# Where the second attention's weights are loaded and split into half-precision parts

## The chip, the cores and the metric

The kernel runs on one core of one Trainium2 chip. The metric is the device time of one execution in microseconds (us); for the kernel before, the median of three runs is given.

## What is computed

Two transformer layers in float32 on an input of 2 x 1024 tokens with 256 features. Each layer adds to x an attention on the layer-normed x, then a feed-forward part on the layer-normed x.

- Layer 0: rotary causal attention with 16 heads of 16; a feed-forward matmul with the signs of its weights.
- Layer 1: causal attention with 16 heads of 128 (`q`, `k`, `v` each with weights and bias per head; scores divided by sqrt(128); output weights `W_O`), and a mixture of 64 experts with a shared expert.

```
q = einsum('bpd,hde->bphe', x, W_Q) + b_Q      # k and v in the same way
scores = einsum('bqhe,bkhe->bhqk', q, k) / sqrt(128)
z = einsum('bkhe,bhqk->bqhe', v, softmax(causal(scores)))
out = einsum('bqhe,hed->bqd', z, W_O) + b_O
```

The change concerns `W_Q`, `W_K`, `W_V` (per head 256 x 384 numbers together, 384 KB) and `W_O` (256 KB for two heads).

## The kernel before, in words

The program is a chain of blocks, built by `build` (L82): load, norm, projections of layer 0 (`l0_qkv`), first attention (`l0_attention`, L477), its output projection, norm, feed-forward, norm, then per batch the second attention (`l1_attention`, L865) and its output projection, then norm, router and experts. In a block each engine has its own list of instructions; engines meet by semaphores. The next block begins when all engines are through with the one before.

**Parts.** The second attention's matmuls are exact to nearly float32 by splitting each operand into two float16 parts: `hi` is the operand rounded to float16, `lo` is the operand minus `hi`. A product takes three matmuls (hi hi, hi lo, lo hi). The query columns of the weights are first multiplied by 1/sqrt(128).

**First attention.** 32 heads (2 batches x 16), taken in pairs. POOL copies a head's query and key parts together (`fetch`, L553) and its values (`fetch_values`, L570). SP turns them by transposing DMAs (`turn`, L595; the maxima's turn at L618). TensorE makes scores twice, once with queries on partitions for VectorE's maxima (L642, L755), once turned (L700) for ScalarE's exponentials (L743). Beside this stand 24 weight jobs of `l1_weights` (L797): 16 for the heads' `W_Q W_K W_V` and 8 for pairs of heads of `W_O`. Head m of the attention carries job m - 4: SP loads the float32 weights (`load`, L834, L840), POOL multiplies the query columns (L823), casts all columns (L829) and subtracts (L831), and SP stores both parts in HBM (`store`, L842, L845). POOL's list in such a head is fetch, values, the job's split, and a store of zeros for a later stage (L589). SP's list is the maxima's turn, the turns for the head after next, the job's store, the load of the next but one job.

**Norm before the second attention** (`norm`, L168, with `l1_buffers`, L1344). SP loads the parts of heads 0 and 1 (L861), the biases and both parts of `W_O` (L1367). POOL sets constants (L1372 to L1374) and scales the biases of two heads (L1379). VectorE normalizes, TensorE turns (L306), ScalarE and VectorE write the two parts of x (L291, L274).

**Second attention, one batch.** 16 heads of 8 steps each, the steps being the 8 blocks of 128 queries in the order 7, 0, 6, 1, 5, 2, 4, 3, with 1 to 8 blocks of keys. A head's steps on the engines:
- TensorE: the scores of the next step (L1052), a sixth of the next head's projections in six of the steps (`prep_pe`, L918: L924, L933), and the products with the values of five steps ago (L1073). The projections read `g.wsplit[par]`, two buffers taken in turn.
- VectorE: the reciprocal of the row sums (L1157), the next maxima (L1144), the `lo` part of a projection (L959, L962), the `lo` part of the probabilities of two steps ago (L1178).
- ScalarE: the `hi` part of a projection (L949, L952), the exponentials (L1125), the `hi` part of the last step's probabilities (L1136).
- POOL: multiplies each step's reciprocals by a constant (L1015); ScalarE's L1136 and VectorE's L1178 read the product `a_rinv`. In the second step it scales the bias of the head after next (L1006) and issues the load of that head's parts (`l1_fetch`, L857, L861).
- SP: turns the probabilities' parts by transposing DMAs (L995).

The buffers' order is that of the lists: POOL starts a step's work only when it is through with the work ahead of it in its list, and ScalarE waits at L1136 for POOL's semaphore `r_ready`. TensorE waits for weights at the first sixth of a head (`w_in`, L1093).

Of the kernel before, what the change touches and what calls it, by code (L numbers as in the profile page):

```python
# [32 lines left out]
ds = bass.ds  # L33
# [48 lines left out]
def build(nc, t_in, out):  # L82
    g = Prog()
    with ExitStack() as ctx:
# [392 lines left out]
def l0_attention(nc, g, w_begin, w_split, w_load, w_store):  # L477
# [32 lines left out]
    with ExitStack() as c:  # L510
# [29 lines left out]
        with nc.Block() as block:  # L540
            @block.gpsimd
            def _(pool):
# [39 lines left out]
                w_begin(pool)  # L582
# [11 lines left out]
            def _(sp):  # L594
# [16 lines left out]
                w_load(sp, 0)  # L611
                w_load(sp, 1)
                for m in range(NH):
# [12 lines left out]
                for i in range(2):  # L626
                    sp.wait_ge(g.s_parts[i], 16 * (WJOBS // 2))

# [165 lines left out]
WJOBS = H + H // 2  # L794


def l1_weights(g, c):  # L797

    g.w1h = g.dram("w1_parts", (H, P, 2, DC * 3 * P), F16)
    g.wo1h = g.dram("wo1_parts", (2, P, H * D), F16)  # L800
    w = [g.sb(f"pw_in{i}", [P, DC * 3 * P], F32, c) for i in range(2)]
    parts = [g.sb(f"pw_part{i}", [P, 2, DC * 3 * P], F16, c) for i in range(2)]
    scale = g.sb("pw_scale", [P, 1], F32, c)
    s_in, s_split, s_set = [g.sem(f"pw_in{i}") for i in range(2)], g.sem("pw_split"), g.sem("pw_set")
    g.s_parts = [g.sem(f"pw_out{i}") for i in range(2)]

    def width(q):
        return DC * 3 * P if q < H else 2 * D

    def done(q):  # L810

        return 3 * min(q, H) + 2 * max(q - H, 0)

    def begin(pool):
        pool.memset(scale[:, :], float(DH1) ** -0.5).then_inc(s_set, 1)
        pool.wait_ge(s_set, 1)

    def split(pool, q):
        n, at = width(q), done(q)
        pool.wait_ge(s_in[q % 2], 16 * (q // 2 + 1))  # L820
        if q < H:
            wq = w[q % 2].rearrange("p (c n) -> p c n", c=DC)[:, :, 0:P]
            pool.tensor_tensor(wq, wq, scale[:, :].unsqueeze(2).to_broadcast([P, DC, P]), ALU.mult).then_inc(s_split, 1)  # L823
            pool.wait_ge(s_split, at + 1)
            at += 1
        if q >= 2:

            pool.wait_ge(g.s_parts[q % 2], 16 * (q // 2))
        pool.tensor_copy(parts[q % 2][:, 0, 0:n], w[q % 2][:, 0:n]).then_inc(s_split, 1)  # L829
        pool.wait_ge(s_split, at + 1)  # L830
        pool.tensor_tensor(parts[q % 2][:, 1, 0:n], w[q % 2][:, 0:n], parts[q % 2][:, 0, 0:n],  # L831
                           ALU.subtract).then_inc(s_split, 1)

    def load(sp, q):  # L834
        if q >= 2:

            sp.wait_ge(s_split, done(q - 1))
        src = g.t["wqkv1"][q].rearrange("p c n -> p (c n)") if q < H else \
            g.t["wo1"][:, 2 * (q - H):2 * (q - H) + 2, :].rearrange("p h n -> p (h n)")
        sp.dma_start(w[q % 2][:, 0:width(q)], src).then_inc(s_in[q % 2], 16)  # L840

    def store(sp, q):  # L842
        sp.wait_ge(s_split, done(q + 1))
        out = g.w1h[q] if q < H else g.wo1h[:, :, (q - H) * 2 * D:(q - H + 1) * 2 * D].rearrange("a p n -> p a n")
        sp.dma_start(out, parts[q % 2][:, :, 0:width(q)]).then_inc(g.s_parts[q % 2], 16)  # L845

    return begin, split, load, store


# [7 lines left out]
def l1_fetch(g, eng, n, par, first):  # L857

    sem = g.sem("a1_w_first") if first else g.sem(f"a1_w{par}")
    head = n % H if isinstance(n, int) else n  # L860
    eng.dma_start(g.wsplit[par].rearrange("p a c n -> p (a c n)"),  # L861
                  g.w1h[ds(head, 1)].rearrange("o p a n -> (o p) (a n)")).then_inc(sem, 16)


def l1_attention(nc, g, b):  # L865
# [16 lines left out]
    w_first, w_in = g.sem("a1_w_first"), [g.sem(f"a1_w{i}") for i in range(2)]  # L882
# [19 lines left out]
    with ExitStack() as c:  # L902
# [81 lines left out]
        with nc.Block() as block:  # L984
# [14 lines left out]
            def _(pool):  # L999
                def next_weights(n, par):  # L1000

                    pool.wait_ge(g_ready, n * NCH + NCH)
                    ahead = n - (N0 - 2) if isinstance(n, int) else n + (2 - N0)
                    hb = ahead % H if isinstance(n, int) else ahead
                    pool.wait_ge(g_lo, n * NCH + NCH)
                    pool.tensor_tensor(g.bias[par][:, :], g.bqk[:, ds(hb, 1), :].rearrange("p o q -> p (o q)"),  # L1006
# [337 lines left out]
def l1_buffers(nc, g, c2):  # L1344
# [15 lines left out]
    def loads(sp):  # L1360
        for n in range(2):
            l1_fetch(g, sp, n, n, True)
# [689 lines left out]
```

## Time and profile before

| what | us |
|---|---|
| median of 3 runs | 1561.48 |
| runs | 1561.48, 1565.09, 1559.58 |
| span of the profiled execution (first to last instruction) | 1556.1 |
| TensorE busy (PE) | 1394.1, 90% of the span |
| VectorE busy (DVE) | 1047.9, 67% |
| ScalarE busy (ACT) | 814.5, 52% |
| GpSimd busy (POOL) | 374.1, 24% |

The profile gives one execution; its own device time is not listed apart from the span, which leaves out what lies before the first and after the last instruction. PE is TensorE's matmuls, PEld its weight loads, SP the queue that issues most DMAs. Lines such as L831 are those of the kernel before. "idle before" is the time an engine stood still ahead of an instruction, with what ended that wait. The granted clock (PEclk) is 1.00 at 2.4 GHz and 0.50 at 1.2 GHz.

### The profile page before, as it was taken

The numbers are of one execution on the slowest core, as the hardware profiler recorded it, in microseconds if no ns is written. First come the engines' busy times: TensorE is split into PE (matmuls) and PEld (weight loads), VectorE is DVE, ScalarE is ACT, GpSimd is POOL, SyncE is SP. The second block draws the span as 40 slices with busy tenths as digits, with TensorE's granted clock in tenths as the row PEclk, the third lists the DMA queues.
The fourth block names the chain that finished last, engine by engine and source line by source line (L and its number), as shares of the span: only waits on it lengthen the run. The fifth ranks groups of instructions, "written<-read, shape, count | busy, mean of one in ns | idle before, by whom it ended". The sixth has DMA issues, their size and how long they took to land. (4 is left out here: it accounts for less than half of the span.)

```text
span 1556.1 us, 36410 instructions
## 1 busy us (share of the span) xinstructions
PE 1394.1 (90%) x12869; PEld 982.9 (63%) x12869; DVE 1047.9 (67%) x2191; ACT 814.5 (52%) x1682; POOL 374.1 (24%) x796
## 2 busy tenths in 40 slices
PE   3848999999679999999989999999998798799977
PEld 2414555554556777777777677777767745599963
DVE  4856777764778888888822888888882378422228
ACT  1316665655327877777711877787770116222330
POOL 0434665530021111111110101111101000577730
PEclk9969999999889999999999999999999799799985
DMA  3038999872025655565620665566651430599948
GB/s 101 1 68 170 248 246 248 214 160 52 1 79 113 143 138 138 133 142 133 138 59 1 129 141 134 135 142 138 138 128 31 133 95 1 162 290 288 289 135 295
DMA packets 463401, 215.08 MB, mean 138 GB/s; under 512 B 412082, under 2 KB 434448, under 8 KB 463072
## 3 DMA queue, kind: packets, MB, share of 16 engines
q1 hardware_dynamic: 448992, 175.09, 47.0%
q0 software_dynamic: 12000, 36.90, 8.0%
q10 hardware_dynamic: 2336, 2.16, 0.4%
q8 instruction: 39, 0.64, 0.2%
q14 instruction: 34, 0.28, 0.1%
HBM read 81.97 MB, written 31.52 MB: 73 GB/s over the span
## 5 line engine op out<-in xcount | busy, mean ns | idle before, releaser
L1073 PE MATMUL bank<-a_pt,v_part 128*128 128x128 f16 x3456 | 235.3, 220 | 13.9 <-DMA a_pt<-a_ph 8.9
L1136 ACT ACTIVATE a_ph<-a_p,a_rinv 128x1024 f16<-128x1024 f32 (+7 forms) x256 | 198.7, 777 | 79.3 <-POOL a_rinv L1015 75.7
L755 DVE TENSOR_REDUCE a_qh<-bank 128x1 f16<-128x1024 f32 (+7 forms) x256 | 182.3, 755 | 85.0 <-PE bank L645 83.3
L1073 PEld LDWEIGHTS bank<-a_pt,v_part 128*128 128x128 f16 x3456 | 208.9, 98 | 47.2 <-DVE z_part L1163 7.5
L1144 DVE TENSOR_REDUCE a_negm<-bank 128x1 f32<-128x1024 f32 (+7 forms) x256 | 191.7, 749 | 55.9 <-PE bank L1057 55.7
L1052 PE MATMUL bank<-a_k,a_q 128*128 128x512 f16 (+3 forms) x1152 | 228.7, 326 | 0.2
L743 ACT ACTIVATE a_p<-bank 128x1024 f32<-128x1024 f32 (+7 forms) x256 | 157.8, 649 | 128.7 <-PE bank L700 113.3
L1178 DVE SCALAR_TENSOR_TENSOR a_ph<-a_p,a_rinv,a_ph 128x1024 f16<-128x1024 f32 (+7 forms) x256 | 206.8, 808 | 1.7 <-ACT a_ph L1136 1.7
L1125 ACT ACTIVATE a_p<-bank,a_negm 128x1024 f32<-128x1024 f32 (+7 forms) x256 | 189.3, 739 | 21.6 <-DVE a_negm L1144 21.6
L1015 POOL TENSOR_TENSOR a_rinv<-a_rinv,p_scale 128x1 f32<-128x1 f32 x256 | 48.8, 191 | 610.6 <-DVE a_rinv L1157 610.4
L924 PE MATMUL bank<-x_part,wsplit 128*128 128x512 f16 x768 | 186.0, 379 | 4.1 <-PEq L199 1.8
L642 PE MATMUL bank<-a_k,a_q 128*128 128x512 f16 (+3 forms) x384 | 108.6, 340 | 33.8 <-DMA a_k<-a_kh 18.9
L1052 PEld LDWEIGHTS bank<-a_k,a_q 128*128 128x128 f16 x1152 | 99.3, 98 | 60.7 <-ACT a_p L1125 1.2
L700 PE MATMUL bank<-a_qm,a_k 128*128 128x512 f16 (+3 forms) x384 | 112.3, 331 | 6.9 <-ACT a_p L743 5.2
L924 PEld LDWEIGHTS bank<-x_part,wsplit 128*128 128x128 f16 x768 | 69.7, 98 | 71.4 <-issue 4.0
L1760 POOL DMA_INDIRECT x_rows<-token_rows,src x64 | 62.3, 973 | 170.0 <-issue 167.9
L1811 PE MATMUL bank<-x_T,wgu 128*88 128x96 f32 x1024 | 96.1, 247 | 0.7 <-issue 0.7
L933 PE MATMUL bank<-wsplit,x_part 128*128 128x128 f16 x1536 | 95.9, 219 | 0.8 <-DVE a_k L959 0.5
L1811 PEld LDWEIGHTS bank<-x_T,wgu 128*88 128x88 f32 x1024 | 92.6, 158 | 4.4 <-issue 0.9
L933 PEld LDWEIGHTS bank<-wsplit,x_part 128*128 128x128 f16 x1536 | 88.2, 98 | 5.7 <-DVE a_k L959 2.1
L1929 DVE TENSOR_TENSOR x_h<-bank,x_sg 88x192 f32<-88x192 f32 x64 | 22.7, 354 | 94.4 <-ACT x_sg L1888 94.4
L1206 PE MATMUL bank<-wo_part,z_part 128*128 128x256 f16 x768 | 84.2, 273 | 1.7 <-PEq L984 1.7
(206 smaller groups left out, 2230.9 us busy)
## 6 DMA issues: line engine op xcount, KB each, us to landing
wgu<-in_wgu SPq DMA_DIRECT2D x64, 352.0 KB
choice_rows<-zero POOLq DMA_DIRECT2D x24, 512.0 KB, 4.9
c_rows<-choice_rows SPq DMA_DIRECT2D x16, 768.0 KB, 11.2
wsplit<-w_parts POOLq DMA_DIRECT2D x30, 384.0 KB, 3.8
wd<-in_wd SPq DMA_DIRECT2D x64, 176.0 KB
pw_in<-in_wqkv SPq DMA_DIRECT2D x16, 384.0 KB, 4.9
w_parts<-pw_part SPq DMA_DIRECT2D x16, 384.0 KB, 2.9
a_pt<-a_ph SPq DMA_TRANSPOSE x256, 3.0
```

What stands on the lines that cost most here:

```text
L700: ins = pe.matmul(ST[k % 2][:, c4 * 512:c4 * 512 + w_], kT[s][:, kb, :], queries[:, kb * P + c4 * 512:kb * P + c4 * 512 + w_], start=True, ...
L743: act.activation(pT[s][:, off[kb]:off[kb + 1]], ST[k % 2][:, 0:(BT - kb) * P], ACT.Exp).then_inc(e_ready, 1)
L755: dve.tensor_reduce(qh[s][:, i, MC:MC + 1], s1_place(t), AX.X, ALU.max, negate=True).then_inc(m_ready, 1)
L924: ins = pe.matmul(G_ps[k % 2], w[:, a, c_, (k // 2) * P:(k // 2 + 1) * P], g.xs[x_][:, c_, b * S + (k % 2) * 512:b * S + (k % 2 + 1) * 512 ...
L933: ins = pe.matmul(G_ps[k % 2][:, j * P:(j + 1) * P], g.xs[x_][:, c_, t * P:(t + 1) * P], w[:, a, c_, 2 * P:3 * P], start=(c_ == 0 and (a, ...
L1052: ins = eng.matmul(ps[:, c4 * 512:c4 * 512 + w_], qT[par][a][:, i * P:(i + 1) * P], kT[par][k_][:, c4 * 512:c4 * 512 + w_], start=(a, k_) ...
L1073: ins = eng.matmul(Z_ps[:, cols], g.vs[par][v_][:, k, :], turned[slot][:, a * blocks[j] + k, :], start=(k == 0 and (v_, a) == PARTS[0]), s ...
L1125: eng.activation(probs[j % NBUF][:, 0:w_], S_ps[j % 4][:, 0:w_], ACT.Exp, bias=negm[:, par, j:j + 1], accum_out=rsum[:, par, j:j + 1]).the ...
L1136: eng.activation(parts[slot][:, 0:w_], probs[slot][:, 0:w_], ACT.Copy, scale=rinv[:, p_, jj:jj + 1]).then_inc(p_hi, 1)
L1144: eng.tensor_reduce(negm[:, par, j:j + 1], S_ps[j % 4][:, 0:blocks[j] * P], AX.X, ALU.max, negate=True).then_inc(m_ready, 1)
L1178: eng.scalar_tensor_tensor(parts[slot][:, w_:2 * w_], probs[slot][:, 0:w_], rinv[:, p_, jj:jj + 1], parts[slot][:, 0:w_], ALU.mult, ALU.su ...
L1811: ins = pe.matmul(b_[:, m * C:(m + 1) * C], g.wgu[s][:, c_, m * MH:(m + 1) * MH], xeT[(s // 2) % 2][:, s % 2, c_, :], start=(c_ == 0), sto ...
```

## The change

The 24 weight jobs leave the first attention, with the two tensors in HBM that held the parts. The second attention loads the float32 weights itself and splits them on POOL. Two raw buffers `g.wraw` (float32, 384 KB each) and one `g.woraw` (256 KB) are new.

- In the norm before the second attention POOL issues the loads of heads 0 and 1 and of the first pair of `W_O`, splits both heads, issues the loads of heads 2 and 3, and scales the biases. SP loads only the biases.
- In the second attention POOL, behind the product of step j of head n, splits slice j of head n + 2, for the first six steps. A slice is 128 of the 768 columns: a cast and a subtraction, and in slices 0 and 3 (query columns) a product first. In the first eight heads of the first batch, steps 6 and 7 split each one half of a pair of `W_O`. After the eighth step POOL scales the bias of head n + 2 and issues the load of head n + 4, and in the first heads that of the next pair of `W_O`.
- TensorE waits for the slices' semaphore `s_wready` in place of the DMA's.
- POOL's loop over pairs of heads is written out.

```diff
-                with ExitStack() as cw:
-                    l0_attention(nc, g, *l1_weights(g, cw))
+                l0_attention(nc, g)
...
                 for m in range(4, NH):
                     fetch(m)
                     fetch_values(m - 2)
-                    if m - 4 < WJOBS:
-                        w_split(pool, m - 4)
...
                     if m + 2 < NH:
                         turn(m + 2)
-                    if 0 <= m - 3 < WJOBS:
-                        w_store(sp, m - 3)
-                        if m - 1 < WJOBS:
-                            w_load(sp, m - 1)
...
+def l1_fetch(g, eng, n):
+
+    eng.dma_start(g.wraw[n % 2][:, :], g.t["wqkv1"][n % H].rearrange("p c n -> p (c n)")).then_inc(g.s_wraw[n % 2], 16)
+
+
+def l1_split(g, pool, n, k):
+
+
+    c_, part = divmod(k, 3)
+    raw = g.wraw[n % 2][:, k * P:(k + 1) * P]
+    dst = [g.wsplit[n % 2][:, a, c_, part * P:(part + 1) * P] for a in range(2)]
+    if k == 0:
+        pool.wait_ge(g.s_wraw[n % 2], 16 * (n // 2 + 1))
+    if part == 0:
+        pool.tensor_tensor(raw, raw, g.bscale[:, 0:1].to_broadcast([P, P]), ALU.mult).then_inc(g.s_wsc, 1)
+        pool.wait_ge(g.s_wsc, DC * n + c_ + 1)
+    pool.tensor_copy(dst[0], raw).then_inc(g.s_whi, 1)
+    pool.wait_ge(g.s_whi, 3 * DC * n + k + 1)
+    pool.tensor_tensor(dst[1], raw, dst[0], ALU.subtract).then_inc(g.s_wready, 1)
...
             @block.gpsimd
             def _(pool):
...
+                for n in range(N0, N0 + H):
                     for j in range(BT):
...
+                        pool.wait_ge(r_raw, n * BT + (j + 1))
+                        pool.tensor_tensor(rinv[:, n % 2, j:j + 1], rinv[:, n % 2, j:j + 1], g.pscale[:, :],
+                                           ALU.mult).then_inc(r_ready, 1)
+                        if n + 2 < B * H and j < 3 * DC:
+                            if j == 0:
+
+                                pool.wait_ge(g_ready, (n + 1) * NCH)
+                            l1_split(g, pool, n + 2, j)
+                        if b == 0 and n < OJOBS and j >= 3 * DC:
+                            l1_split_out(g, pool, n, j - 3 * DC)
+                    if n + 2 < B * H:
+
+                        pool.wait_ge(g_lo, (n + 1) * NCH)
+                        pool.tensor_tensor(g.bias[n % 2][:, :], g.bqk[:, (n + 2) % H, :], g.bscale[:, :],
+                                           ALU.mult).then_inc(b_ready, 1)
+                    if n + 4 < B * H:
+                        pool.wait_ge(g.s_wready, 3 * DC * (n + 3))
+                        l1_fetch(g, pool, n + 4)
+                    if b == 0 and n + 1 < OJOBS:
+                        pool.wait_ge(g.s_wosplit, 4 * (n + 1))
+                        l1_fetch_out(g, pool, n + 1)
...
-                            if k == 0 and which == "first" and b == 0:
-                                eng.wait_ge(w_first, 32)
-                            elif k == 0:
-
-                                eng.wait_ge(w_in[1 - par], n * 8 + (8 - 8 * (1 - par)))
+                            if k == 0:
+                                eng.wait_ge(g.s_wready, n * (3 * DC) + 2 * 3 * DC)
...
     def loads(sp):
-        for n in range(2):
-            l1_fetch(g, sp, n, n, True)
         sp.dma_start(g.bqk[:, :, :], g.t["b_QK"]).then_inc(s_in, 16)
         sp.dma_start(g.bv[:, :], g.t["b_V"]).then_inc(s_in, 16)
         sp.dma_start(g.bo[:, :], g.t["b_O"].partition_broadcast(P)).then_inc(s_in, 16)
-        for a in range(2):
-            sp.dma_start(g.wo1p[a].rearrange("p h n -> p (h n)"), g.wo1h[a]).then_inc(s_wo, 16)
-        sp.wait_ge(s_wo, 32)
+        sp.wait_ge(s_in, 48)
...
         pool.wait_ge(s_set, 3)
 
+        for n in range(2):
+            l1_fetch(g, pool, n)
+        l1_fetch_out(g, pool, 0)
+        for n in range(2):
+            for k in range(3 * DC):
+                l1_split(g, pool, n, k)
+        pool.wait_ge(g.s_wready, 2 * 3 * DC)
+        for n in range(2):
+            l1_fetch(g, pool, n + 2)
         pool.wait_ge(s_in, 48)
```

## Rows read from the trace of the kernel before

**Rows 1.** Busy time by stretch: length; PE, PEld, DVE, ACT, POOL; clock; DMA.

```profile
117.00:335.00 218.00, 203.01 (x2035) 108.62 (x2033) 155.23 (x271) 131.20 (x218) 120.47 (x243) 1.00 0.93 223
...
470.00:800.00 330.00, 320.20 (x3544) 235.50 (x3543) 270.71 (x506) 252.14 (x506) 36.30 (x160) 0.99 0.60 134
```

**Rows 2.** Waits in steady heads of the second attention, first batch, 500 to 745.

```profile
ACT a_ph L1136 <- POOL a_rinv L1015: 30.2, 24, 1.4
DVE a_negm L1144 <- PE bank L1057: 21.4, 36, 0.9
...
POOL wsplit L861 <- issue: 5.6, 12, 0.7
```

**Rows 3.** Waits in the first attention, 117 to 335, then SP's queue's own.

```profile
PE bank L700 <- DMA a_qm<-a_qh: 0.3, 1, 0.3
...
SPq L845 <- POOL pw_part L831: 2.0, 5, 0.5
```

**Rows 4.** Timeline of ScalarE: first exponential of three heads, two pairs apart.

```profile
303.25 1.02 ACT L743 ACTIVATE a_p<-bank 128x1024 f32<-128x1024 f32 x1 [0.23 <-PE bank L700]
...
337.30 1.02 ACT L743 ACTIVATE a_p<-bank 128x1024 f32<-128x1024 f32 x1 [0.23 <-PE bank L700]
...
371.23 1.02 ACT L743 ACTIVATE a_p<-bank 128x1024 f32<-128x1024 f32 x1
```

**Rows 5.** Timeline of the norm before the second attention and the first matmul behind.

```profile
443.00 0.10 POOL L1372 MEMSET bscale<- 128x1 f32 x1 [4.44 <-POOLq L1313]
...
450.86 0.58 POOL L1379 TENSOR_TENSOR bias<-bqk,bscale 128x2 f32<-128x2 f32 x2 [7.70 <-DMA bo<-in_b_O]
...
451.51 6.02 DVE L274 TENSOR_TENSOR x_part<-bank,x_part 128x256 f16<-128x256 f32 x16
...
457.85 1.46 PE L924 MATMUL bank<-x_part,wsplit 128*128 128x512 f16 x6 [1.80 <-PEq L199]
```

**Rows 6.** POOL's DMAs of line 861: issue (ns), and time to landing.

```profile
L861 POOL DMA_DIRECT2D wsplit<-w_parts x30: 563/563/585, 471.6 to 1116.6; - x30
...
DMA to landing us min/median/max: 2.9/3.8/5.4
```

**Rows 7.** POOL's groups by shape: busy us, mean ns, idle before.

```profile
L823 POOL TENSOR_TENSOR pw_in<-pw_in,pw_scale 128x256 f32<-128x256 f32 x16 | 9.7, 607 | 26.5 <-DMA pw_in<-in_wqkv 26.5
...
L831 POOL TENSOR_TENSOR pw_part<-pw_in,pw_part 128x512 f16<-128x512 f32 x8 | 9.2, 1151 | 0.7
...
L575 POOL COPY a_vh<-v 128x128 f32<-128x128 f32 x32 | 9.1, 286 | 66.7 <-PE bank L663 66.7
```

**Rows 8.** Timeline of POOL in one weight job.

```profile
205.90 0.82 POOL L829 CAST pw_part<-pw_in 128x768 f16<-128x768 f32 x1
206.81 1.64 POOL L831 TENSOR_TENSOR pw_part<-pw_in,pw_part 128x768 f16<-128x768 f32 x1
```

**Rows 9.** Busy time by stretch, as rows 1, and TensorE's timeline at 787.98.

```profile
456.30:459.70 3.40, 1.85 (x9) 0.91 (x10) 1.13 (x4) 0.73 (x3) 0.00 (x0) 1.00 0.03 7
...
787.40:790.80 3.40, 2.82 (x27) 2.85 (x28) 1.08 (x2) 0.00 (x0) 0.00 (x0) 0.50 0.92 208
...
787.98 1.33 PE L1073 MATMUL bank<-a_pt,v_part 128*128 128x128 f16 x11 [2.76 <-DMA a_pt<-a_ph]
```

**Rows 10.** Timeline of VectorE in a steady head.

```profile
575.42 0.15 DVE L1157 RECIPROCAL a_rinv<-a_rsum 128x1 f32<-128x1 f32 x1
...
576.35 0.34 DVE L1178 SCALAR_TENSOR_TENSOR a_ph<-a_p,a_rinv,a_ph 128x128 f16<-128x128 f32 x1
...
577.44 0.56 DVE L1144 TENSOR_REDUCE a_negm<-bank 128x1 f32<-128x384 f32 x1 [0.68 <-PE bank L1057]
```

**Rows 11.** Line 428 on VectorE (ns min/median/max), one instance, POOL's line 459 beside it.

```profile
L428 DVE TENSOR_TENSOR qk_parts<-rot,qk_parts x32: 411/422/1491, 42.7 to 90.1; 128x256 f16<-128x256 f32 x32
...
87.66 1.48 DVE L428 TENSOR_TENSOR qk_parts<-rot,qk_parts 128x256 f16<-128x256 f32 x1
...
87.48 1.37 POOL L459 TENSOR_TENSOR rot<-rot 128x512 f32<-128x512 f32 x1 [1.82 <-DVE rot L442]
```

More of the change, by code:

```diff
@@ L621, in _ @@
                         turn(m + 2)
-                    if 0 <= m - 3 < WJOBS:
-                        w_store(sp, m - 3)
-                        if m - 1 < WJOBS:
-                            w_load(sp, m - 1)
-                for i in range(2):
-                    sp.wait_ge(g.s_parts[i], 16 * (WJOBS // 2))
             def max_scores(pe, t, m, s):
@@ L789, in _ @@
                 z_out(NP - 1, NH - 2)
[L794 to L847, printed above, removed]
+OJOBS = H // 2
 LAG = 5
@@ L854, with l1_fetch_out, l1_split_out @@
 NCH = 6
[L857 to L862, printed above, removed]
+def l1_fetch(g, eng, n):
[12 more added lines that the diff above has]
+    pool.tensor_tensor(dst[1], raw, dst[0], ALU.subtract).then_inc(g.s_wready, 1)
+def l1_fetch_out(g, eng, q):
+    eng.dma_start(g.woraw[:, :], g.t["wo1"][:, 2 * q:2 * q + 2, :].rearrange("p h n -> p (h n)")).then_inc(g.s_wo, 16)
+def l1_split_out(g, pool, q, k):
+    raw = g.woraw[:, k * D:(k + 1) * D]
+    dst = [g.wo1p[a][:, 2 * q + k, :] for a in range(2)]
+    if k == 0:
+        pool.wait_ge(g.s_wo, 16 * (q + 1))
+    pool.tensor_copy(dst[0], raw).then_inc(g.s_wosplit, 1)
+    pool.wait_ge(g.s_wosplit, 4 * q + 2 * k + 1)
+    pool.tensor_tensor(dst[1], raw, dst[0], ALU.subtract).then_inc(g.s_wosplit, 1)
 def l1_attention(nc, g, b):
@@ L881, in l1_attention @@
     pt_in = [g.sem(f"a1_turned{i}") for i in range(NBUF)]
-    w_first, w_in = g.sem("a1_w_first"), [g.sem(f"a1_w{i}") for i in range(2)]
     N0 = b * H
@@ L999, in _ @@
             def _(pool):
[L1000 to L1006, printed above, removed]
-                                       g.bscale[:, :], ALU.mult).then_inc(b_ready, 1)
-                    l1_fetch(g, pool, hb, par, False)
@@ L1010, in head @@
-                def head(eng, n, par, which, more):
-                    for j in range(BT):
-                        if j == 1 and more:
-                            next_weights(n, par)
-                        eng.wait_ge(r_raw, n * BT + (j + 1))
-                        eng.tensor_tensor(rinv[:, par, j:j + 1], rinv[:, par, j:j + 1], g.pscale[:, :],
-                                          ALU.mult).then_inc(r_ready, 1)
-                head(pool, N0, 0, "first", True)
-                head(pool, N0 + 1, 1, "first", True)
@@ L1020, in _ @@
-                with pool.Fori(1, H // 2 - 1) as pair:
-                    for par in range(2):
-                        head(pool, pair * 2 + (N0 + par), par, "mid", True)
-                for par in range(2):
-                    head(pool, N0 + H - 2 + par, par, "last", b + 1 < B)
+                for n in range(N0, N0 + H):
+                    for j in range(BT):
+                        pool.wait_ge(r_raw, n * BT + (j + 1))
[17 more added lines that the diff above has]
+                        l1_fetch_out(g, pool, n + 1)
@@ L1357, in l1_buffers @@
     g.bvp = g.sb("bv_part", [P, 2, H], F16, c2)
-    s_in, s_set, s_wo, b_ready = g.sem("l1_in"), g.sem("l1_set"), g.sem("l1_wo"), g.sem("a1_bias")
+    g.wraw = [g.sb(f"w_raw{i}", [P, DC * 3 * P], F32, c2) for i in range(2)]
+    g.woraw = g.sb("wo_raw", [P, 2 * D], F32, c2)
+    g.s_wraw = [g.sem(f"a1_w_in{i}") for i in range(2)]
+    g.s_wsc, g.s_whi, g.s_wready = [g.sem(f"a1_w_{n}") for n in ("scaled", "hi", "ready")]
+    g.s_wo, g.s_wosplit = g.sem("l1_wo"), g.sem("l1_wo_split")
+    s_in, s_set, b_ready = g.sem("l1_in"), g.sem("l1_set"), g.sem("a1_bias")
     def loads(sp):
-        for n in range(2):
-            l1_fetch(g, sp, n, n, True)
         sp.dma_start(g.bqk[:, :, :], g.t["b_QK"]).then_inc(s_in, 16)
```

11 lines of the change are left out of this document (3 added, 8 removed).

## The prediction

> **What bounds the kernel now.** I read the stages first (busy time by stretch), then the waits inside the two attentions, then the timeline where the change sits. Times below are of the one profiled execution, span 1556.1 us; the median of the runs is 1561.48 us, 5.4 us more. That rest (launch and end) is taken as unchanged, so a difference found in the profile is added to 1561.48. A difference under 0.3% (4.7 us) cannot be told from none here: the three runs alone spread over 5.5 us.
>
> TensorE is the limit of both attentions: busy 203.0 of 218 us while the first one carries the weight jobs, and 320.2 of 330 us in the first batch of the second [rows 1]. In the second attention's steady heads the list of waits has no TensorE entry at all; what waits is ScalarE for POOL's `a_rinv` (30.2 us in 24 waits over 12 heads) and VectorE for TensorE's scores (21.4 us, 1.8 us a head) [rows 2]. Those two are slack behind a saturated TensorE. So work moved between POOL, SP and the DMA queues changes the time only if it makes TensorE wait, or stands in the short norm between the FFN and the second attention, where TensorE has little to do.
>
> **First attention: jobs removed.** Gone are 24 loads and 24 stores on SP, 16 products, 24 casts and 24 subtractions on POOL. None was in TensorE's way: it waited once, 0.3 us, for a turned maximum, and SP's queue waited for POOL's splits 2.0 us in all [rows 3]. What the jobs cost is read from the pace. Two pairs of heads with jobs start at 303.25 and end at 337.30, 34.05 us; the next two, without, run to 371.23, 33.93 us [rows 4]. That is 0.06 us a pair, over 12 pairs 0.7 us at most if all carry it. I take -0.3 us; bounds 0 and -1.1 (a few turned maxima landed late early in the stage). The zero-filling stores of POOL's queue stay; they are issued earlier, because POOL no longer waits for a job's load ahead of them.
>
> **Norm before the second attention: work added.** Before, SP fetches ready parts and POOL has three memsets and two bias products. After, POOL issues three DMAs, splits two heads (6 slices each), issues two more DMAs and makes the biases, all inside the norm's block; the next block starts when every engine is through. The prices:
> - POOL starts at 443.0 [rows 5]; three memsets and their wait, 0.2 us.
> - Landing: a POOL DMA of 384 KB takes 0.563 us to issue and 2.9 to 5.4 us, median 3.8, to land [rows 6]. First weights at 443.2 + 3.8 = 447.0. The other two land behind it, under cover of head 0's slices.
> - A slice has 128 columns. Cast: the 128x128 copy, 0.29 us. Subtraction: 1.64 us for 768 columns (206.81) and 1.15 us for 512 give 0.49 us per 256, so 0.41 us for 128. Product: 0.61 us for 256 less 0.25, 0.36 us. From a cast's end (205.90 + 0.82) to the subtraction that waits for it at 206.81 is 0.09 us [rows 7, 8].
> - A head: 6 x 0.29 + 6 x 0.41 + 2 x 0.36 = 4.92 us, six such gaps and two behind products +0.7, less about 0.4 where a subtraction's end and the next cast, which wait for nothing, overlap (estimate); so 5.2 us; two heads 10.5 us. Splits end at 457.5.
> - Two DMA issues 1.1 us, two bias products 0.6 us [rows 5]: POOL ends at 459.2.
>
> VectorE ended this norm at 457.53 and TensorE started at 457.85 [rows 5], so the change of blocks takes 0.3 us. POOL becomes last, by 1.7 us: TensorE starts at about 459.5. Bounds: landing at 446.1, no gaps and cheap slices give +0.3 us; landing at 448.6, slices a tenth dearer and 0.4 us before each of five issues (12 issues idled 5.6 us in the steady heads) give +6.2 us [rows 2, 6]. I take +1.7, since each term has a row of its own size.
>
> What this trace has of such landings was 2.9 to 5.4 us [rows 6]. The Trainium skill's page "DMA: Bandwidth & Descriptors", section on the anatomy of one SWDGE DMA, fits 2.0 us plus bytes over 436 GB/s for a DMA from GpSimd's queue. By that estimate 384 KB takes 2.9 us, the rows' lowest and not their median, and the start would be 0.9 us late instead of 1.7.
>
> **TensorE's clock after the longer pause.** Before, TensorE stops at 456.05, starts again 1.80 us later and is at 2.4 GHz from 456.3 to 459.7 [rows 5, 9]. With the start at 459.5 the pause becomes 3.5 us. After a pause of 2.76 us near the end of the first batch the clock stood at 1.2 GHz from 787.4 to 790.8 [rows 9]. I expect the same here: 3.4 us at half rate lose 1.7 us of matmul work, of which 0.3 us hides in waits for evacuation; +1.4 us. Bounds 0 (no fall) and +3.4 (two such stretches).
>
> **Second attention: slices beside the heads.** Before, a head has on POOL 8 `a_rinv` products, one bias and one DMA. After, for 30 heads six slices (0.8 us, or 1.2 with the product) come on top, one behind each of the first six `a_rinv`; in the first eight heads two half slices of the output weights (1.1 us) and a DMA. Who waits for POOL's queue is ScalarE, at the next `a_rinv`. VectorE's reciprocals come closest around the 128-column instance of line 1178: one starts at 575.42, the next follows that instance, which ends at 576.69 [rows 10]. In these 1.2 us slice 2 (0.8 us) fits. Behind the last `a_rinv` of the first eight heads half slice, bias and two issues need some 3.7 us against 2.0 us to the next reciprocal, so the next head's first `a_rinv` comes about 1.7 us late; ScalarE has 2.5 us a head of waiting for POOL to give (30.2 by 12) [rows 2]. New weights are ready a whole head (some 20 us: 330 by 16 [rows 1]) before TensorE asks, so the new wait costs nothing. In steady heads: 0 us. In the last head of the first batch TensorE does wait, for turned probabilities; slices there may delay VectorE by 0.1 to 0.4 us. I take +0.3, bounds 0 and +1.0.
>
> **Sum:** -0.3 + 1.7 + 1.4 + 0.3 = +3.1 us, 1564.6 us.
>
> **Rivals.**
> (A) The slices stall VectorE. The trace has such a stall: the subtraction of line 428, both inputs in SBUF, takes 0.41 us by itself and 1.48 us when it starts at 87.66 in the middle of POOL's 87.48 to 88.85; it ends at 89.14, 0.29 us after POOL's end [rows 11]. Line 1178, eight times a head, has two SBUF inputs as well. By my replay of one head, slice 2's subtraction (576.2 to 576.6) meets the one that starts at 576.35 and holds it by 0.1 us; the half slices of the first eight heads hold two more, 0.5 us together. VectorE's next idle gap, 0.68 us at 577.44, takes the first up [rows 10]. The point that decides is 1.8 us a head: with more stall than VectorE's idle time, scores come late. If none of it were absorbed, 30 x 0.1 + 8 x 0.5 = 7 us come on top: 1571.6. For it speaks the stall, against it the idle gap behind each collision. Chance 0.13.
> The Trainium skill's page "SBUF — State Buffer", section "Who interferes with whom", has the same stall as a rule: the read port that both engines use is locked for a whole instruction. It speaks against this change, and for cutting the work into slices.
> (B) The first attention gains more. All that could be won is TensorE's 15.0 us of idle time there [rows 1]; a third of it would be -5 us and, with a norm that costs +0.3, give 1556.8. Against it: those gaps alternate with VectorE and ScalarE, and the pairs without jobs keep the pace [rows 4]. Chance 0.07.
> (C) The norm hides POOL's work after all (early landing, no fall of the clock): -0.3 + 0.3 + 0.3 = +0.3, 1561.8. Chance 0.20.
> (D) My forecast, 1564.6: chance 0.60; its own range 1560 to 1569.
>
> **How the numbers follow.** The lows sum to -0.8 us and the highs without (A) to +10.6 us; with the scatter of a median of a few runs the range is 1559.5 to 1570. Faster by over 0.3% is (B), 0.07. Slower by over 0.3% is (A) with its 0.13 and the upper end of (D), where landing and clock both go badly, 0.13: 0.26. The rest, 0.67, is no change that can be told.
>
> **What the new profile would show.** Right: pairs in the first attention still 17 us apart; TensorE's first matmul of the second attention 1 to 3 us later after the norm's start, with POOL the last engine in the norm; 1.2 GHz granted for some 3 us at that start; heads as far apart as before with no TensorE wait; line 1178 instances 0.1 to 0.4 us longer at places. Wrong: TensorE waiting for scores' evacuation in the steady heads, heads longer by 0.1 us or more, a start more than 6 us late, or pairs below 16.8 us.

## The result and the profile after

The kernel after takes 1587.71 us (median of four runs, 1587.25 to 1588.44) against 1562.57 us of the kernel before (four runs): ratio 1.0168, 95% interval 1.0149 to 1.0186. Forecast was 1564.6, range 1559.5 to 1570. The profiled span grew from 1556.1 to 1585.8 us, by 29.7. That is 4.6 us more than the medians differ. Where a run lists both, its time is 1.6 to 1.9 us above its span, so the profiled execution of the kernel before was faster than any of its four timed runs. Differences of stages, taken from the profiles, overstate the loss by these 4.6 us. The head of the page after:

```profile
span 1585.8 us, 36456 instructions
...
PE 1404.9 (89%) x12869; PEld 984.9 (62%) x12869; DVE 1053.6 (66%) x2191; ACT 815.4 (51%) x1682; POOL 489.7 (31%) x1221
```

GpSimd carries 116 us more than before, but it is idle two thirds of the span; what the kernel lost is TensorE standing still or running slowly. Five stages, cut at the same instructions in every kernel, show where. "First attention" runs from its first GpSimd memset to the first exponential of its last head; "norm" from the norm's first VectorE instruction to TensorE's first matmul of the second attention; "start" from there to the first exponential; heads 1 and 2 of the first batch; "tail" from the first exponential of that batch's last head to the second batch's first. "Total" is the timed median, the rest are us of the profiled execution.

| kernel | total | span | first attention | norm | start | heads 1, 2 | tail |
|---|---|---|---|---|---|---|---|
| before | 1562.57 | 1556.1 | 287.4 | 14.8 | 11.6 | 20.2, 20.2 | 86.0 |
| after | 1587.71 | 1585.8 | 298.7 | 23.0 | 13.8 | 21.5, 21.4 | 90.5 |
| e1_spacers | 1574.36 | 1572.6 | 287.6 | 21.8 | 13.2 | 20.2, 21.8 | 90.8 |
| e2_zeros_early | 1578.02 | 1576.2 | 286.0 | 23.0 | 14.0 | 21.7, 21.9 | 91.3 |
| e3_fetch_later | 1580.87 | 1579.1 | 296.5 | 18.8 | 14.0 | 21.7, 21.7 | 88.8 |
| e4_tail_fetch | 1581.29 | 1579.5 | 296.0 | 22.5 | 13.7 | 21.6, 21.7 | 86.0 |
| e5_wo_moved | 1583.95 | 1582.1 | 296.3 | 22.6 | 14.0 | 20.2, 21.0 | 90.3 |
| e6_head1_later | 1576.22 | 1574.4 | 297.1 | 15.7 | 11.6 | 20.2, 21.5 | 90.8 |
| e7_all_moved | 1560.89 | 1559.8 | 285.3 | 15.7 | 13.2 | 20.8, 20.7 | 86.0 |
| e8_before_in_twos | 1568.45 | 1566.8 | 294.6 | 14.8 | 11.6 | 20.2, 20.2 | 85.9 |
| e9_even_stores | 1576.94 | 1575.2 | 286.0 | 23.1 | 14.0 | 21.6, 21.8 | 90.9 |
| e10_odd_stores | 1576.47 | 1574.7 | 286.6 | 22.9 | 13.9 | 21.6, 21.6 | 90.4 |
| e11_all_moved_2 | 1568.1 | 1565.3 | 285.8 | 15.5 | 12.9 | 20.5, 20.1 | 90.1 |
| e13_before_zeros_early | 1559.8 | 1557.0 | 285.2 | 14.4 | 12.9 | 20.2, 20.2 | 86.3 |

e7, e11 and e13 were run 12, 6 and 12 times, e1 to e6 and e8 to e10 once each, beside a kernel before of 1564.33 us (e1 to e4), 1563.21 us (e5, e6) and 1560.87 us (e8 to e10). From before to after: first attention +11.3, norm +8.2, start +2.1, heads 1 and 2 +2.5, tail +4.5, together 28.6; the other 1.1 us is for the most part the scatter of code that is the same in both (the first stages alone +1.2). Where the code of the first attention is that of after (after, e3 to e6), it took 296.0 to 298.7 us, so a difference under 3 us means little there: in the profile of after one odd head took 13.5 us where the others took 10.1 to 10.4, and 1.2 GHz stood from 155.0 to 158.4; e3 to e6 have no such head. The totals of e1, e3, e4, e5 and e6 came out 1 to 3 us below what was expected of them; in e3 to e6 the first attention alone gave 1.6 to 2.7 us against the profile of after.

Busy time by stretch in the kernel after, columns as [rows 1]: the two attentions, then the start of the second and the tail of its first batch.

```profile
118.10:346.00 227.90, 205.95 (x2024) 107.98 (x2022) 154.31 (x269) 131.19 (x216) 55.99 (x178) 0.99 0.68 143
...
492.00:822.00 330.00, 316.98 (x3496) 231.23 (x3494) 273.85 (x505) 252.58 (x506) 137.86 (x423) 0.99 0.64 140
...
472.40:482.70 10.30, 4.59 (x11) 1.61 (x12) 0.75 (x1) 0.69 (x1) 1.92 (x6) 0.50 0.23 79
813.80:820.60 6.80, 4.79 (x45) 4.19 (x41) 0.00 (x0) 0.00 (x0) 0.00 (x0) 0.50 0.71 157
```

TensorE's idle time in the first attention went from 15.0 us [rows 1] to 22 (227.90 less 205.95), although the DMA share there fell from 0.93 to 0.68. In the last two stretches the granted clock is 0.50 (1.2 GHz).

**First attention.** Waits of the kernel after, 117 to 345 (us in total, times, longest):

```profile
POOL a_qh L563 <- DMA a_k<-a_kh: 94.0, 14, 10.5
...
DVE a_qh L743 <- PE bank L633: 70.2, 89, 3.5
...
PE bank L630 <- DMA a_k<-a_kh: 9.1, 11, 2.3
```

TensorE now waits 9.1 us for turned keys, in 11 waits. The kernel before has one such wait of 1.7 us (its 117 to 335; it stands beside the turned maximum of [rows 3]):

```profile
PE bank L642 <- DMA a_k<-a_kh: 1.7, 1, 1.7
```

What changed is when the 512-KB zero stores leave GpSimd. The timeline before, then after (start, issue time):

```profile
198.78 0.59 POOL L589 DMA_DIRECT2D choice_rows<-zero  x1
...
208.39 0.59 POOL L589 DMA_DIRECT2D choice_rows<-zero  x1
...
218.10 0.59 POOL L589 DMA_DIRECT2D choice_rows<-zero  x1
```

```profile
201.23 0.53 POOL L585 DMA_DIRECT2D choice_rows<-zero  x1
...
203.39 0.53 POOL L585 DMA_DIRECT2D choice_rows<-zero  x1
...
219.20 0.53 POOL L585 DMA_DIRECT2D choice_rows<-zero  x1
```

Before, one store per head, here 9.6 and 9.7 us apart. After, two 2.2 us apart and then a pause: before an even head's values GpSimd waits for TensorE, and the odd head has nothing of that kind. The weight jobs had held the second store back. SyncE's transposes of the odd head meet both; DMA issues of the kernel after, then of e9 (half of the stores), 160 to 325, KB each and median us to landing:

```profile
choice_rows<-zero POOLq DMA_DIRECT2D x18, 512.0 KB, 5.3
a_qm<-a_qh SPq DMA_TRANSPOSE x18, 3.9
a_q<-a_qh SPq DMA_TRANSPOSE x18, 5.2
a_k<-a_kh SPq DMA_TRANSPOSE x18, 4.4
```

```profile
choice_rows<-zero POOLq DMA_DIRECT2D x10, 512.0 KB, 4.5
a_qm<-a_qh SPq DMA_TRANSPOSE x20, 3.8
a_q<-a_qh SPq DMA_TRANSPOSE x20, 4.2
a_k<-a_kh SPq DMA_TRANSPOSE x19, 3.8
```

The medians are over even and odd heads: in the kernel after an even head's query transpose lands in 3.3 us, an odd head's in 7.1, with one store (e9) in 5.0. TensorE waits for the key transpose, the last of three. From 130 to 335 us it had landed 5.8 to 6.6 us after SyncE began the first of the three in an even head, and in an odd head 9.1 to 9.4 us (once 10.9). With one store it was 7.3 to 8.5 (e9) and 7.6 to 8.9 (e10). TensorE waited for turned keys in each of the eleven odd heads of the kernel after and in none of e9 and e10. From the even head's first exponential to the odd head's it is 10.1 to 10.4 us in the kernel after (once 13.5) and 9.1 to 9.4 in the kernel before: this is the odd head's time in the expectations below.

**Norm.** GpSimd's timeline in the kernel after, then TensorE's, then the block-end instruction of GpSimd's queue (ns min/median/max, start):

```profile
455.42 0.10 POOL L1331 MEMSET p_scale<- 128x1 f32 x1
457.76 1.15 POOL L793 DMA_DIRECT2D w_raw<-in_wqkv  x2 [2.24 <-issue]
...
461.26 0.50 POOL L805 TENSOR_TENSOR w_raw<-w_raw,bscale 128x128 f32<-128x128 f32 x1 [1.71 <-DMA w_raw<-in_wqkv]
...
472.50 0.43 POOL L809 TENSOR_TENSOR wsplit<-w_raw,wsplit 128x128 f16<-128x128 f32 x1
473.23 1.12 POOL L793 DMA_DIRECT2D w_raw<-in_wqkv  x2 [0.30 <-POOL wsplit L809]
474.36 0.36 POOL L1345 TENSOR_TENSOR bias<-bqk,bscale 128x2 f32<-128x2 f32 x2
```

```profile
478.11 1.44 PE L887 MATMUL bank<-x_part,wsplit 128*128 128x512 f16 x3 [8.83 <-PEq L198]
```

```profile
L198 POOLq DRAIN  x1: 4110/4110/4110, 473.7 to 473.7; - x1
```

GpSimd stands still for 2.24 us ahead of its first DMA, splits until 472.93, and its drain lasts from 473.7 to 477.8: the second of the two fetches begun at 473.23 (its own issue at 473.81) lands 3.77 us later, at 477.58. VectorE's own part had ended at 470.76.

**Steady heads.** Waits over twelve heads, 552 to 794; they answer to [rows 2]:

```profile
ACT a_ph L1091 <- POOL a_rinv L966: 27.0, 22, 1.4
DVE a_negm L1099 <- PE bank L1015: 19.8, 30, 0.9
```

27.0 and 19.8 us, against 30.2 and 21.4. The heads stay 20.18 to 20.47 us apart. VectorE's `lo` parts of the probabilities did get longer at three of their eight widths (mean 989 ns against 874 at 640 columns, 672 against 607 at 384, 380 against 342 at 128), some 0.2 us a head, and the heads did not.

### The profile page after: what moved, and what is told of

It is laid out like the page before. It is cut to its first block and busy times, and to the rows that moved or that the text cites. A ratio compares the mean times of both kernels' runs of the same rounds, so it can differ in the third digit from the quotient of the medians.

```text
span 1585.8 us, 36456 instructions
## 1 busy us (share of the span) xinstructions
PE 1404.9 (89%) x12869; PEld 984.9 (62%) x12869; DVE 1053.6 (66%) x2191; ACT 815.4 (51%) x1682; POOL 489.7 (31%) x1221
## 5 line engine op out<-in xcount | busy, mean ns | idle before, releaser
L1031 PE MATMUL bank<-a_pt,v_part 128*128 128x128 f16 x3456 | 236.5, 220 | 18.0 <-DMA a_pt<-a_ph 10.5
L1134 DVE SCALAR_TENSOR_TENSOR a_ph<-a_p,a_rinv,a_ph 128x1024 f16<-128x1024 f32 (+7 forms) x256 | 211.1, 825 | 1.7 <-ACT a_ph L1091 1.7
L1080 ACT ACTIVATE a_p<-bank,a_negm 128x1024 f32<-128x1024 f32 (+7 forms) x256 | 189.2, 739 | 21.4 <-DVE a_negm L1099 21.4
L887 PEld LDWEIGHTS bank<-x_part,wsplit 128*128 128x128 f16 x768 | 70.3, 98 | 79.8 <-issue 13.9
L809 POOL TENSOR_TENSOR wsplit<-w_raw,wsplit 128x128 f16<-128x128 f32 x192 | 83.1, 433 | 15.4
```

Of the source, the lines that this page charges most:

```text
L887: ins = pe.matmul(G_ps[k % 2], w[:, a, c_, (k // 2) * P:(k // 2 + 1) * P], g.xs[x_][:, c_, b * S + (k % 2) * 512:b * S + (k % 2 + 1) * 512 ...
L1031: ins = eng.matmul(Z_ps[:, cols], g.vs[par][v_][:, k, :], turned[slot][:, a * blocks[j] + k, :], start=(k == 0 and (v_, a) == PARTS[0]), s ...
L1080: eng.activation(probs[j % NBUF][:, 0:w_], S_ps[j % 4][:, 0:w_], ACT.Exp, bias=negm[:, par, j:j + 1], accum_out=rsum[:, par, j:j + 1]).the ...
L1134: eng.scalar_tensor_tensor(parts[slot][:, w_:2 * w_], probs[slot][:, 0:w_], rinv[:, p_, jj:jj + 1], parts[slot][:, 0:w_], ALU.mult, ALU.su ...
```

## The experiments

All but e8 and e13 start from the kernel after. Theory Z: zero stores in pairs. Theory N: GpSimd's chain and drain in the norm. Theories W and T: raw fetches that meet the transposes of the probabilities, in heads 1 and 2 and in the tail. The expectations of e1 and e2 count the first attention up to the norm's first instruction: 351.3 us before, 362.2 after.

**e1_spacers.** GpSimd's splits (product, cast, subtraction) come back on a buffer of ones, without their loads and stores.

```
+                w_begin(pool)
                 for m in range(4, NH):
                     fetch(m)
                     fetch_values(m - 2)
+                    w_split(pool, m - 4)
                     pool.dma_start(zv[m - 4], g.zero[:, :])
```

> The kernel after, with GpSimd's 24 splits put back into the first attention on a buffer of ones, without their loads, stores and load waits (their results are used by nobody). Theory Z (the zero stores now leave GpSimd in pairs about 2.2 us apart, where the splits held them 8 to 10 us apart, and meet the transposing DMAs of the odd heads): the splits space the stores again, so the odd heads' transposes land in 3.2 to 3.6 us instead of 5 to 7, and the first attention goes from 362.2 us back to 351 to 353; total 1577 to 1579. Rival L (the splits' loads and stores, or the waits on them, kept something else in order, or the first attention is longer for a reason that has nothing to do with the stores): the first attention stays at 360 to 364 us and the total at 1585 to 1589. Rival G (GpSimd time is scarce): slower than the kernel after.

First attention 287.6 us (352.6 up to the norm), total 1574.36, 2.6 us under the expected range. Doing useless work is 13 us faster than doing none, 11 of it in this stage: what the jobs gave the kernel before was the distance between stores. Spaced stores still meet transposes, which from 175 us on take up to 5.2 us to land and not only 3.2 to 3.6, but TensorE waits for none of them there. L falls, G too.

**e2_zeros_early.** The stores go to the QKV projection.

```
                 for t in range(NT):          # l0_qkv, GpSimd
                     ...
+                    for z in range(2 * t, min(2 * t + 2, ZD)):
+                        pool.dma_start(zv[z], g.zero[:, :]).then_inc(g.s_zero, 16)
```

> The kernel after, with the 24 zero stores issued from GpSimd's loop of the first QKV projection (two per token tile) in place of the first attention. Theory Z: no store is left to meet the transposes, so the first attention goes from 362.2 us to 349 to 351.5 (a head pair of 17.85 us falls to 17.0 or less), the QKV stage grows by 0 to 2 us, total 1575 to 1578. Rival L (not the stores): the first attention stays at 360 to 364 us, total 1585 to 1589.

286.0 us (351.0 up to the norm), with the QKV stage no longer (the first attention begins at 92.89, after: 92.93). The stores, not the jobs' removal in itself, cost the 11 us.

**e3_fetch_later.**

```
-        pool.wait_ge(g.s_wready, 2 * 3 * DC)     # scales(), in the norm
-        for n in range(2):
-            l1_fetch(g, pool, n + 2)
+                if b == 0:                        # l1_attention, GpSimd, first thing
+                    pool.wait_ge(g.s_wready, 2 * 3 * DC)
+                    for n in range(2):
+                        l1_fetch(g, pool, n + 2)
```

> The kernel after, with the two fetches of heads 2 and 3 moved out of the norm's GpSimd list to the beginning of the second attention's. Theory N (the norm's end waits in GpSimd's drain for these two fetches to land, 473.7 to 477.8 us): the 1.1 us of issuing and the 3.1 us of the drain go, the stretch from the norm's first VectorE instruction to the first attention matmul falls from 23.0 to 18.5 to 20 us, total lower by 3 to 4.5 us (1583 to 1585). Rival M (the drain waits for something else, or the matmul for the biases): 23.0 us as before, total unchanged at 1587 to 1589.

Norm 18.8 us, 4.2 less: theory N, M falls. The total was 6.8 us lower; 2.2 of it is the scatter of the first attention, 1.7 the tail, whose code is the same.

**e4_tail_fetch.** Head 19's raw fetch waits for the second batch.

```
-                    if n + 4 < B * H:
+                    if n + 4 < B * H and n != H - 1:
...
+                if b == 1:
+                    pool.wait_ge(g.s_wready, 3 * DC * (H + 2))
+                    l1_fetch(g, pool, H + 3)
```

> The kernel after, with the last raw fetch of batch 0 (head 19's, issued 810.7 us, landing 5.1 us later) moved to the start of the second batch's GpSimd list. Theory T (that fetch meets the last transposes of the probabilities of batch 0): from head 15's first exponential to the second batch's first, 90.5 us falls to 86 to 87, total lower by 3.5 to 4.5 us (1583 to 1584.5). Rival U (the tail's extra time is the GpSimd slices, or the clock alone): 90 to 91 us, total unchanged. Rival V (the fetch meets the second batch's first transposes instead): 90.5 us falls, but the first heads of the second batch take 1 to 4 us more.

Tail 86.0 us, as before, and the second batch's heads unchanged: theory T. The fetch, 16.2 us into the last head, meets two transposes of the probabilities: they take 5.3 and 5.1 us to land, the same two in e4 2.7 and 3.0. The waits of TensorE's matmuls in the tail, after (806 to 828), then e4 (804 to 826):

```profile
PE bank L1031 <- DVE z_part L1118: 2.9, 2, 2.4
...
PE bank L1031 <- DMA a_pt<-a_ph: 2.8, 2, 2.0
```

```profile
PE bank L1034 <- DMA a_pt<-a_ph: 3.4, 2, 2.6
...
PE bank L1034 <- DVE z_part L1121: 0.6, 1, 0.6
```

Together 5.7 us against 4.0. The other 2.8 us of the 4.5 go with the clock: 1.2 GHz was granted for 10.2 us of the kernel after's tail (two stretches, 813.8 to 820.6 and 824.0 to 827.4, with 8.2 us of matmuls in them), for 3.4 us of e4's and of the kernel before's (3.0 and 2.8 us of matmuls). What such a fall costs was not tried apart from the waits.

**e5_wo_moved.**

```
-                    if b == 0 and n + 1 < OJOBS:      # end of head n
+                        if b == 0 and 0 < n < OJOBS and j == 2:
                             l1_fetch_out(g, pool, n)
```

> The kernel after, with the fetch of the output weights (256 KB) issued behind the third block of a head in place of directly behind the 384-KB fetch at the end of the head before. Theory W (heads 1 and 2 of the first batch take 21.4 to 21.5 us because two fetches 0.6 us apart meet the transposes of the head's first blocks): both return to 20.2 to 20.6 us, total lower by 1.5 to 2.6 us. Rival X (one fetch alone at that place is enough, or the loop's first passes are the cause): both stay above 21.2 us. Rival Y (the moved fetch meets other transposes): heads 1 and 2 fall, but heads 3 to 7 rise above 20.6 us each.

Head 2 takes 21.0 us; in every run without this edit that splits in the second attention it took 21.4 to 21.9. Head 1's 20.2 proves less, since it was also 20.2 in e1 and e6. Part of W, then: the 384-KB fetch alone keeps some of the cost. Nor does the place of the fetches alone decide it: heads 3 to 7 of the kernel after have the same two, also 2.4 and 3.0 us behind the head's first exponential, and take 20.2 to 20.5 us. What differs is how late a transpose of the probabilities lands. Head 1 (508 to 520), then head 3 (551 to 563), of the kernel after:

```profile
DMA to landing us min/median/max: 2.3/3.9/7.4
```

```profile
DMA to landing us min/median/max: 2.4/3.1/6.0
```

With 7.4 us TensorE stood still for 1.1 us; with 6.0 to 6.4 us (heads 3 to 7) it had no pause of 0.2 us. In head 1 of e1 and e6, whose fetches stand at the same place, the longest took 5.9 and 6.1 us. Why the same fetches delay the transposes of heads 1 and 2 more is open.

**e6_head1_later.**

```
-        for n in range(2):                        # scales()
-            for k in range(3 * DC):
-                l1_split(g, pool, n, k)
+        for k in range(3 * DC):
+            l1_split(g, pool, 0, k)
+                if b == 0:                        # l1_attention, GpSimd, first thing
+                    for k in range(3 * DC):
+                        l1_split(g, pool, 1, k)
+                    pool.wait_ge(g.s_wready, 2 * 3 * DC)
+                    for n in range(2):
+                        l1_fetch(g, pool, n + 2)
```

> The kernel after, with the norm's GpSimd list cut to head 0's slices: head 1's six slices and the fetches of heads 2 and 3 move to the beginning of the second attention's list. Theory N (GpSimd's chain of landing, twelve slices, two issues and a drain sets the norm's end): 5.8 us of slices and the 4 us of the fetches go from it, until VectorE's own part ends last; from the norm's first VectorE instruction to the first attention matmul 23.0 us falls to 15 to 17 us (before: 14.8), and the matmul stands at 468 to 472 in place of 478.1 with an undisturbed first attention counted as after's; total lower by 6 to 9 us. Rival M (the matmul waits for something else at the norm's end): 20 us or more. Rival P (head 1's slices now hold up the start of the attention): the norm falls, but from the matmul to the first exponential, 13.75 us, it rises by 2 us or more, or head 0 takes over 18 us.

Norm 15.7 us, start 11.6, head 0 16.6 us long (after: 17.1): theory N again, without P. GpSimd, VectorE and TensorE at the end of this norm:

```profile
467.64 0.35 POOL L1347 TENSOR_TENSOR bias<-bqk,bscale 128x2 f32<-128x2 f32 x2
```

```profile
464.54 5.83 DVE L273 TENSOR_TENSOR x_part<-bank,x_part 128x256 f16<-128x256 f32 x16
```

```profile
470.69 1.02 PE L887 MATMUL bank<-x_part,wsplit 128*128 128x512 f16 x4 [1.93 <-PEq L198]
```

GpSimd is through at 468.0 and VectorE at 470.37, as it was last in [rows 5]. The 0.9 us over the kernel before lies in VectorE's 16 normalizing instructions, here and in the kernel before (busy us, mean ns):

```profile
L265 DVE TENSOR_SCALAR n_xnb<-x,mean,rstd 128x256 f32<-128x256 f32 x16 | 6.4, 472 | 0.0
```

```profile
L266 DVE TENSOR_SCALAR n_xnb<-x,mean,rstd 128x256 f32<-128x256 f32 x16 | 5.3, 406 | 0.0
```

They take 0.40 to 0.41 us (once 0.47) until GpSimd's first split begins at 461.23, and 0.51 to 0.65 us beside the splits; GpSimd's casts take 0.37 to 0.49 us there and 0.29 later. So the slices did meet VectorE, in the norm. This is read from the timeline; no run kept the two apart.

**e7_all_moved** is e2, e4, e5 and e6 together.

> The kernel after with four edits together: zero stores in the QKV projection, head 1's slices and the fetches of heads 2 and 3 behind the norm, the output weights' fetch behind the third block of a head, the last raw fetch of batch 0 at the start of the second batch. If the four meetings and waits are all of the loss: first attention 286 us from its start to the last head's first exponential, norm as in the kernel before to within 2 us, heads 1 and 2 at 20.2 to 20.6, tail of batch 0 at 86, total 1558 to 1566 us, a ratio to the kernel before of 0.997 to 1.002. If something else remains, or the parts meet again elsewhere: 1567 us or more. If less GpSimd and DMA work in the first attention was worth something in itself: below 1558.

1560.89 us (12 runs) against 1563.21 (17 runs), ratio 0.9987, interval 0.9973 to 1.0001. Heads 1 and 2, at 20.8 and 20.7, stay above the expected range. The 25 us are gone, and what is left cannot be told from the kernel before.

**e8_before_in_twos** starts from the kernel before.

```
-                    if m - 4 < ZD:
-                        pool.dma_start(zv[m - 4], g.zero[:, :])
+                    if m - 4 < ZD and m % 2:
+                        for z in (m - 5, m - 4):
+                            pool.dma_start(zv[z], g.zero[:, :])
```

> The kernel before, untouched but for its zero stores: the store of an even head waits for the odd head's and the two leave together, behind the odd head's split. Theory Z in its burst form (two 512-KB stores at once are what slows a transposing DMA): the transposes that meet a pair land in 5 to 7 us, and the first attention grows from 287.4 us (its start to the last head's first exponential) by 3 to 11 us. Theory Z in its phase form (what counts is that a store leaves GpSimd just as SyncE begins an odd head's transposes; behind the splits it falls between two heads): unchanged to 1 us, 287 to 289 us.

294.6 us, 7.2 more, with nothing else of the change in it; one head of it took 11.9 us, with 1.2 GHz from 251.1 to 254.5. The cost is uneven: the first pairs of stores fall between transposes and cost nothing, from 240 us on they meet them (key transpose issued at 240.9: 8.7 us to landing, and TensorE waited 2.8 us for it). So both forms hold a part: it takes two stores, and they must meet the transposes.

**e9_even_stores, e10_odd_stores.** Half of the stores stay in the first attention, the other half goes to the QKV projection.

```
-                    if m - 4 < ZD:
+                    if m - 4 < ZD and m % 2 == 0:     # e10: m % 2 == 1
```

> The kernel after with half of its zero stores: the twelve of the odd heads are issued in the QKV projection, the twelve of the even heads (the first of each pair) stay. Burst form: no two stores meet, so the odd heads take 9.3 to 9.5 us and the first attention 286 to 288 us. Phase form: one store at that place still slows the odd heads to 9.7 to 10.2 us, first attention 291 to 299 us.

> The kernel after with the other half: the twelve of the even heads are issued in the QKV projection, the twelve of the odd heads (the second of each pair, some 2 us behind the first) stay. Burst form: odd heads 9.3 to 9.5 us, first attention 286 to 288 us. Phase form: 9.7 to 10.2 us, 291 to 299 us; if this run is long and that with the even stores is not, the phase is that of the second store, on top of the query and key transposes.

286.0 and 286.6 us. Each store of a pair is free by itself at the place where the two cost 0.9 us a head: burst, not phase.

**e11_all_moved_2** is e7 with both fetches of a head inside the next one.

```
+                        if n and n + 3 < B * H and j == 2:
+                            l1_fetch(g, pool, n + 3)
+                        if b == 0 and 0 < n < OJOBS and j == 4:
+                            l1_fetch_out(g, pool, n)
```

> As the run with four edits together, but both fetches of a head are issued inside the next head: the raw weights behind its third block, the output weights behind its fifth (the last raw fetch of batch 0 falls into the second batch by this). If the fetch at a head's first blocks is what is left in heads 1 and 2 (20.7 us each there): 20.2 to 20.4 us each, and the total 1 to 2 us below the 1560.9 of that run, ratio to the kernel before 0.996 to 0.999. If not: heads 1 and 2 at 20.6 or more, total as there.

Heads 1 and 2 at 20.5 and 20.1, but 1568.1 us, ratio 1.0041 (1.0025 to 1.0058): a miss. The tail is 90.1 us and the second batch's first two heads take 2.3 us more than in e7. The fetch in the first batch's last head, at 778.7, now meets that head's transposes, and the clock falls to 1.2 GHz three times between 785 and 803. A place that is free in a steady head is not free in a first or last one.

**e13_before_zeros_early** is the kernel before with e2's edit.

> The kernel before with its 24 zero stores issued in the QKV projection; the weight jobs stay. If the stores, spaced by the splits, cost the kernel before nothing: first attention 287 to 287.6 us, total unchanged, ratio 0.999 to 1.001, and what the run with four edits has over the kernel before comes from the weight jobs' removal. If they cost something there too: first attention 285 to 286.5 us, ratio 0.998 to 0.9995, and moving them is worth as much without the change.

First attention 285.2 us; 1559.8 us, ratio 0.9989 (0.9976 to 1.0003). Spaced stores may cost the kernel before some 2 us, at the edge of what can be told. With the weight jobs in place it is as fast as e2's and e7's first attention without them.

## Why the prediction was wrong

- **First attention, -0.3 us: wrong, and the largest error.** The failing step is the sentence that the zero-filling stores "stay; they are issued earlier", priced at nothing. Issued earlier meant issued in twos; measured +11.3 us in the profiles (8.6 to 9.7 in e3 to e6), and e1, e2, e8, e9 and e10 put it on the pairs. The bounds, 0 and -1.1, held no loss at all, since only removed instructions were priced and not what their waits did to the DMAs behind them. That the jobs themselves cost TensorE nothing was right: with the stores away, 285.2 us with jobs (e13) and 286.0 without (e2). Rival (B) falls with it. The reading that TensorE waited once, 0.3 us, left out the wait of 1.7 us for turned keys at 127.3, the kind that grew to 9.1.
- **Norm, +1.7 (0.3 to 6.2): right that GpSimd becomes last, mis-sized at +8.2.** Splits were priced at 10.5 us and took 11.7, the first ones slowed beside VectorE (e6). Left out were the 2.24 us ahead of the first DMA, and the landing of the two fetches issued last: the sum has "two DMA issues 1.1 us", but the block ends when they have landed, 4.1 us of drain, most of it waiting. e3 takes the fetches out for 4.2 us, e6 the second head's slices too for 7.3. The first landing took 3.43 us, inside the bounds taken. The Trainium skill's page "DMA: Bandwidth & Descriptors", section on the anatomy of one SWDGE DMA, gave 2.9 us by estimate; the run is 0.5 us above it.
- **Clock, +1.4 (0 to 3.4): the size held at +2.1, in part by luck.** TensorE's pause was 8.83 us, not 3.5, and 1.2 GHz stood from 472.4 to 482.7, over the first 4.6 us of matmuls. That the pause brings this is not shown. The kernel before had 1.2 GHz from 446.1 to 456.3, in the norm; that ended 1.5 us ahead of the first matmul. In e13, with the same code there and the same pause, it stood until 460.2, 2.9 us past the first matmul, and the start took 12.9 us in place of 11.6. So up to 1.3 of the 2.1 us may be scatter. A longer pause does go with a longer start: 13.2 to 14.0 us in the eight kernels that paused for 4.6 us or more, 11.6 to 13.2 in the six with 1.8 to 2.0. But e6 and e7 have the same norm and nearly the same pause (1.93 and 2.00 us), and their starts took 11.6 and 13.2 us. What decides was not settled.
- **Steady heads, 0: right.** Rival (A) would have shown as heads longer by 0.1 us or more; but for four fetch-laden ones (20.3 to 21.5 us) they kept to 20.2. The stall itself is there, 0.2 us a head, and VectorE had the idle time for it.
- **Heads 1 and 2: missing.** The half slices and issues were counted on GpSimd's clock, where there is slack. The two fetches as traffic, 640 KB within 0.6 us beside the transposes that TensorE waits for, were not: +2.5 us. e5 and e11, which move them, take most of it away; why heads 3 to 7 bear the same traffic is open.
- **Tail, +0.3 (0 to 1.0): wrong cause.** The slices were blamed in advance; it was the fetch at 810.7, issued in the head where TensorE waits for transposes, and the clock that fell with it: +4.5 us, undone by e4.
- **The rest of 5.4 us.** The prediction took median less span as launch and end. That is 1.6 to 1.9 us in every run that lists both; the other 3.6 us were the scatter of the one profiled execution.

## What to carry to other kernels

A job that is taken away takes its waits with it, and these may have been spacing somebody's transfers: list the DMAs behind each removed wait and ask when they leave now, and what is in flight then. A moved load is priced three times: as instructions, as traffic beside the transfers that the bottleneck waits for, and by where its landing falls, above all at the end of a block. Where the removed work was hidden, as here, there is little to gain; the best arrangement found only gave the loss back.

## What was not expected of the hardware

- One 512-KB store raised an odd head's transposes from 3.3 to about 5 us to landing (e9: the query's to 4.9 to 5.1, in one head 6.3; e10: the key's to 4.9 to 6.3) and cost nothing; a second one 2.2 us behind the first raised the query's to 7.0 to 7.3 us and cost the head 0.9 us (after).
- GpSimd's end of a block waited for DMAs of its own queue whose data nobody in that block needs: drain 4.11 us with two fetches behind the splits, 1.10 us without (e3, e6).
- VectorE's normalizing instructions (128x256) took 0.51 to 0.65 us in place of 0.41 beside GpSimd's 128-column splits, and the splits' casts 0.37 to 0.49 in place of 0.29 (after, e6).
- GpSimd idled 2.2 to 2.4 us between the norm's last memset and its first DMA (after, e6). The trace has an 8-KB read of the instruction queue at 456.1, inside that gap; whether it is the cause was not tried.
